# Row statistics of the second normalisation taken in the attention stage; the gelu output weighted by POOL and DVE, a tile each

## The reference

```
h = concatenate([tokens(x), text(x_txt)], axis=1)          # 64 x 228 x 192
h = h + attn(layernorm(h))
h = h + ffn(layernorm(h))

def ffn(x): return bitlinear(gelu(bitlinear(x, w1, g1)), w2, g2)
def bitlinear(x, w, g):
    xn = x * rsqrt(mean(x * x) + 1e-6) * g
    scale = 127 / max(max(|xn|), 1e-5)                    # one per row
    xq = clip(round(xn * scale), -128, 127) / scale
    return xq @ ternary(w)
```

## Time and profile before

| | |
|---|---|
| median of 3 runs | 1896.07 us |
| the profiled execution | 1889.4 us, of which the span from first to last instruction is 1887.7 us |
| busy, share of the span | PE 1579.8 us (84%), DVE 1364.8 (72%), ACT 1283.7 (68%), POOL 1089.7 (58%) |
| mean granted clock of TensorE | 0.880 of full speed (2.4 GHz) |

### The profile page before, as it was taken

One profiled execution on the slowest core, in us unless ns is written; L12 is line 12 of the kernel. 1 busy time (PEld: TensorE's weight loads), 2 busy tenths in 40 slices (PEclk: granted clock), 3 DMA queues, 4 the chain that ended last, 5 costly groups with the idle time before them and its releaser, 6 DMA issues.

```text
span 1887.7 us, 50796 instructions
## 1 busy us (share of the span) xinstructions
PE 1579.8 (84%) x16574; PEld 1297.6 (69%) x16574; DVE 1364.8 (72%) x3151; ACT 1283.7 (68%) x1958; POOL 1089.7 (58%) x1503
## 2 busy tenths in 40 slices
PE   0539999999999999999999999999466666666666
PEld 0427788888888888888888888887345555555555
DVE  3636676767767676767676767676389999999996
ACT  1226666766767676767676666665288888888887
POOL 5035555555555555555555555554177777777775
PEclk9869999999999999999999999999666666666665
DMA  8674666665657565756565666660000000000000
GB/s 102 141 127 59 95 87 96 86 99 83 103 79 104 83 99 83 99 88 94 89 94 91 91 93 88 94 87 25 17 16 21 21 21 22 22 22 22 22 22 26
DMA packets 159967, 132.96 MB, mean 70 GB/s; under 512 B 32558, under 2 KB 151040, under 8 KB 159808
## 3 DMA queue, kind: packets, MB, share of 16 engines
q1 hardware_dynamic: 159168, 131.00, 44.4%
q0 software_dynamic: 768, 1.57, 0.5%
HBM read 118.32 MB, written 11.91 MB: 69 GB/s over the span
## 4 chain that ended last, share of the span: by engine, by line
PE 66%; DVE 15%; issue 7%; SPq 3%; ACT 3%; DMA 3%; POOL 1%; DVEq 1%; ACTq 0%; POOLq 0%
PE ps L1092 20%; PE ps L1176 8%; PE ps L1259 7%; PE ps L1250 7%; PE ps L1206 4%; DVE ff_st L860 4%; PE ps L1238 3%; PE ps L1232 3%; PE ps L1211 3%; PE ps L1336 2%; PE ps L1355 2%; DVE xpix L841 2%; PE ps L1167 2%; DVE xpix L853 1%; PE ps L1157 1%
## 5 line engine op out<-in xcount | busy, mean ns | idle before, releaser
L1092 PE MATMUL ps<-w_eff,pix 118*112 118x193 f32 (+1 forms) x2048 | 408.4, 337 | 25.0 <-ACT pix L909 24.3
L927 ACT ACTIVATE probs<-ps,isw 116x688 f32<-116x688 f32 x384 | 299.2, 831 | 171.6 <-PE ps L1238 171.6
L527 POOL TENSOR_TENSOR xpix<-probs,g_b 112x192 f32<-112x192 f32 (+1 forms) x512 | 296.5, 609 | 109.1 <-ACT probs L1044 99.7
L741 DVE TENSOR_REDUCE nmax<-ps 116x12 bf16<-116x1344 f32 (+2 forms) x192 | 299.6, 1560 | 80.2 <-PE ps L1211 77.7
L452 POOL TENSOR_TENSOR xsq<-xsq 118x784 f32<-118x784 f32 (+2 forms) x192 | 221.8, 1155 | 218.5 <-ACT xsq L920 208.4
L1092 PEld LDWEIGHTS ps<-w_eff,pix 118*112 118x112 f32 (+1 forms) x2048 | 309.8, 167 | 52.4 <-issue 18.9
L472 POOL TENSOR_SCALAR_AFFINE_SELECT probs<-probs 116x464 f32<-116x464 f32 x384 | 268.2, 717 | 46.5 <-ACT probs L927 31.0
L909 ACT ACTIVATE pix<-xpix 118x896 f32<-118x896 f32 (+1 forms) x128 | 198.4, 1552 | 104.9 <-DMA xpix<-in_x 56.0
L457 POOL TENSOR_TENSOR front_st<-front_st,expo 128x2 f32<-128x2 f32 x64 | 45.0, 703 | 235.2 <-DVE front_st L693 221.2
L1336 PE MATMUL ps<-w1t,xpix 96*112 96x384 f16 (+1 forms) x512 | 160.7, 488 | 14.6 <-ACT xpix L1035 13.3
L685 DVE TENSOR_SCALAR front_st<-ps 112x1 f32<-112x1 f32 (+1 forms) x128 | 18.3, 151 | 213.8 <-PE ps L1157 202.4
(11 more groups left out here) (161 smaller groups left out, 3363.3 us busy)
## 6 DMA issues: line engine op xcount, KB each, us to landing
xpix<-in_x SPq DMA_DIRECT2D x192, 196.0 KB
xpix<-in_x SPq DMA_DIRECT2D x192, 195.1 KB
rden<-den_rows SPq DMA_DIRECT2D x256, 85.5 KB, 2.1
out<-xpix SPq DMA_DIRECT2D x64, 87.0 KB
out<-xpix SPq DMA_DIRECT2D x64, 84.0 KB
xpix<-in_x SPq DMA_DIRECT2D x128, 34.1 KB
xpix<-in_x SPq DMA_DIRECT2D x128, 34.0 KB
den<-o_sb SPq DMA_DIRECT2D x256, 2.7 KB
```

Source lines behind the costliest of these rows:

```text
L527: last = nc.gpsimd.tensor_tensor(v2[0:P, b, tile, cols], gel[0:P, b, tile, cols], g2_b[0:P, cols], ALU.mult)
L741: V.tensor_reduce(dst, src, AX_X, ALU.max, negate=True).then_inc(s_mx, 1)
L927: A(probs[0:TB, g, 2 * e:2 * e + 2, :], ps[0:TB, 4 + 2 * e:6 + 2 * e, 0:SK], ACT.Exp, scale=isw[0:TB, 7:8]).then_inc(s_p, 1)
L1092: last = MM(ps_tok[tile][0:P, :], src, w_eff[0:HI, o, :], start=(o == 0), stop=(o == OFFS - 1))
```

## The change

Four things:

1. The statistics of the second normalisation (mean, variance, peak) move from DVE's FFN step to DVE's attention step: a new function `measure(n - 1)` stands behind the third round of maxima. Mean, root and peak are kept for all images, two columns each. POOL takes the root in its own attention step (`row_roots`). Between the stages DVE makes `scale1` and `step1` of all images at once, in five instructions.
2. In the FFN stage DVE centres the rows again (`centre`) and quantises them with the kept scale.
3. The product of gelu and g2 of tile 0 goes from POOL to DVE (`weigh`); POOL keeps tile 1. The second quantisation of tile 1 goes from ACT to DVE (`quantise_second`); ACT keeps tile 0. POOL takes over the addition of epsilon to the mean squares (`gelu_roots`).
4. DVE's order in a step is now: centre i+1, final i-3, weigh i, peaks of i-1, quantise i+1, scales of i-1, quantise tile 1 of i-1.

Buffers move with it: `v1` uses the SBUF of `tok_t`, `bias_q` that of `aT`. The core of the diff:

```diff
+            def measure(n):
+                ...
+                dve.wait_ge(s_h2, n + 1)
+                apart(dve)
+                for tile, P in enumerate((TA, TB)):
+                    last = V.bn_stats(ln_st[0:P, 20 + 6 * tile:26 + 6 * tile], h_all[0:P, hcols(n, tile)])
+                chain(last, 1)
+                ...
+                after(dve, s_rms, n)
+                V.tensor_scalar(ln_st[:, 32:34], ln_st[:, 35:38:2], 1.0 + EPS_RMS,
+                                EPS_LN * EPS_RMS, ALU.mult, ALU.add).then_inc(s_var2, 1)
+                V.tensor_copy(mean2[:, bass.ds(n * 2, 2)], ln_st[:, 34:38:2])
+                for tile, P in enumerate((TA, TB)):
+                    last = V.scalar_tensor_tensor(v1[0:P, tile, :], h_all[0:P, hcols(n, tile)],
+                                                  ln_st[0:P, 34 + 2 * tile:35 + 2 * tile], g1_b[0:P, :],
+                                                  ALU.subtract, ALU.mult)
+                chain(last, 3)
+                for tile, P in enumerate((TA, TB)):
+                    last = V.tensor_reduce(peak[0:P, bass.ds(n * 2 + tile, 1)], v1[0:P, tile, :], AX_X, ALU.max,
+                                           apply_absolute_value=True)
+                last.then_inc(s_peak, 1)
...
+            link(V.tensor_tensor(peak[:, :], rms[:, :], peak[:, :], ALU.mult))
+            link(V.tensor_scalar(peak[:, :], peak[:, :], 1e-5, None, ALU.max))
+            link(V.reciprocal(inv_peak[:, :], peak[:, :]))
+            V.tensor_scalar(step1[:, :], peak[:, :], isw[:, 4:5], None, ALU.mult)
+            link(V.scalar_tensor_tensor(scale1[:, :], inv_peak[:, :], 127.0, rms[:, :], ALU.mult, ALU.mult))
...
+            def quantise_first(n):
+                dve.wait_ge(f_v1, n + 1)
+                after(dve, f_t1, n)
+                for tile, P in enumerate((TA, TB)):
+                    ins = V.tensor_scalar(q1[0:P, tile, :], v1[0:P, tile, :], scale1[0:P, bass.ds(n * 2 + tile, 1)],
+                                          MAGIC16, ALU.mult, ALU.add)
+                ins.then_inc(f_q1, 1)
...
+            def weigh(n, b):
+                for tile, P in ((0, TA),):
+                    after(dve, f_q2[tile], n - 1)
+                    dve.wait_ge(f_g, 2 * n + tile + 1)
+                    V.tensor_tensor(v2[0:P, b, tile, :], gel[0:P, b, tile, :], g2_b[0:P, :],
+                                    ALU.mult).then_inc(f_v2[tile], 1)
+
+            def peaks(n, b):
+                for tile, P in enumerate((TA, TB)):
+                    dve.wait_ge(f_v2[tile], n + 1)
+                    ins = V.tensor_reduce(ff_st[0:P, b, 26 + tile:27 + tile], v2[0:P, b, tile, :], AX_X, ALU.max,
+                                          apply_absolute_value=True)
...
+            def ffn_step(i, b, new=True, mid=True, last_=True, fresh=True):
+
+                if new:
+                    centre(i + 1)
+                if last_:
+                    final(i - 3, 1 - b)
+                if fresh:
+                    weigh(i, b)
                 if mid:
+                    peaks(i - 1, 1 - b)
+                if new:
+                    quantise_first(i + 1)
                 if mid:
+                    second_scales(i - 1, 1 - b)
+                    quantise_second(i - 1, 1 - b)
...
-                          scale=ff_st[0:P, b, 40 + tile:41 + tile]).then_inc(f_g, 1)
+                          scale=step1[0:P, bass.ds(m * 2 + tile, 1)]).then_inc(f_g, 1)
```

More of the change, by code:

```diff
@@ L240, in build @@
         f_sc = sem("quantiser_scales_ready")
[L241 to L242 removed]
+        f_v2 = [sem(f"gelu_weighted{i}") for i in range(2)]
+        f_q2 = [sem(f"second_quantised{i}") for i in range(2)]
         f_t2 = sem("second_transposed")
@@ L509, in _ @@
             step_images(IMAGES - 1, 0, None, newer=False, newest=False)
[L511 to L537, removed]
+            row_roots(IMAGES - 2)
+            row_roots(IMAGES - 1)
+            def weight(n, b):
+                after(pool, f_q2[1], n - 1)
+                pool.wait_ge(f_g, 2 * n + 2)
+                for lo in range(0, HIDDEN, HIDDEN // 4):
+                    cols = slice(lo, lo + HIDDEN // 4)
+                    last = nc.gpsimd.tensor_tensor(v2[0:TB, b, 1, cols], gel[0:TB, b, 1, cols],
+                                                   g2_b[0:TB, cols], ALU.mult)
+                last.then_inc(f_v2[1], 1)
@@ L569, in _ @@
             step(V.memset(nmax[:, :, :], 0.0))
+            for filled in (mean2, rms, peak):
+                step(V.memset(filled[:, :], 1.0))
             dve.wait_ge(s_const, 32)
@@ new lines, in final @@
+            def final(n, b):
+                dve.wait_ge(f_m2, n + 1)
+                after(dve, f_out, 32 * n)
+                for tile, P in enumerate((TA, TB)):
+                    end = V.scalar_tensor_tensor(y[0:P, tile, :], ps[0:P, 1, tile * 256:tile * 256 + DIM],
+                                                 ff_st[0:P, b, 42 + tile:43 + tile], h_all[0:P, hcols(n, tile)],
+                                                 ALU.mult, ALU.add)
+                end.then_inc(f_y, 1)
+            def weigh(n, b):
[4 more added lines that the diff above has]
+                                    ALU.mult).then_inc(f_v2[tile], 1)
@@ L1037, in ffn_step @@
                 if mid:
-                    quantise(i, b, 0)
-                    quantise(i, b, 1)
+                    quantise(j, 1 - b)
                 if new:
-                    after(act, f_v2, 2 * m - 2)
+                    for tile in range(2):
+                        after(act, f_v2[tile], m - 1)
                     for tile, P in enumerate((TA, TB)):
```

185 lines of the change are left out of this document (95 added, 90 removed).

## The result

The changed kernel takes 1919.65 us (median of 4 runs, 1912.34 to 1928.37), the kernel before 1897.02 on the same chip: ratio 1.0118, 95% interval 1.0066 to 1.0170. It is slower, as forecast (1924). The profiled execution is 1912.34 us, with a span of 1910.6 against 1887.7.

The account below looks back on a forecast made before the run. The prediction took PE to bound attention and DVE the FFN stage, where the change would close a chain of 8.4 us an image: + 26 us, + 2 for scales, giving 1917 profiled, 1924 median; own range 1905 to 1940, wider range 1882 to 1944.

Parts of the forecast that it names:

- What leaves DVE: FFN stage: second-normalisation statistics leave, a product and a quantisation come; DVE busy falls from 7.33 to 6.8 us an image.
- The closed chain: FFN stage: first quantisation, PE, gelu, weighing, peaks, next first quantisation form one loop; 8.4 us an image against 7.97.
- The correction to the mean clock: FFN chain: PE's parts taken at the stretch's mean times, lowering 8.60 us by 0.30 and 0.14 to 8.16.
- the 8.60 of the one image: FFN chain priced from one traced image, PE almost throughout at the lower clock: 4.75 + 0.98 + 0.95 + 1.92 us.
- The rival that the clock rises: FFN stage: PE at 2.4 GHz shortens the chain to 6.6 us, DVE's 7.2 bounds, 1850 us; chance 0.04.
- the rival above it: FFN stage: DVE stays the bound at 7.45 us an image, 1866 us; chance 0.18.
- The signs named beforehand: FFN profile: period 8.2 to 8.6 us, DVE about 80% busy waiting mainly on gelu, PE waiting for L883, longer ACT wait.
- No change: FFN stage: the chain comes out at the present period of 7.97 us, 1898 us; chance 0.08.
- DVE-bound: FFN stage: DVE's busy time and gaps still bound, so its lost work shows, 1866 us; chance 0.18.
- Contention: FFN stage: a 0.6 us POOL piece delays weighing or first quantisation, 1961 us; attention overrun alone 1936; chance 0.13.
- Attention hidden: Attention stage: DVE's added 2.8 us an image fits its 3.1 us idle time, 0.3 to spare; cost 0.
- The scales of all rows: End of the attention stage: five DVE instructions making scales for all images at once, not hidden, + 2 us.

Follow-up runs that it names:

- the order tests: The changed kernel with the first quantisation of image i+1 ahead of the weighing: 1824.85 us; with it between weighing and peaks: 1823.50 us.
- the doubled weighing: The changed kernel with DVE making the weighing product twice, first into memory nobody reads: 1989.42 us, ratio 1.0507.
- the doubled centring: The changed kernel with DVE centring image i+1 twice, first into memory nobody reads: 1926.63 us, ratio 1.0184.
- the first trace: Profile of the unaltered changed kernel in its first measurement of four runs; the profiled execution took 1912.34 us.
- the second trace of after: Profile of the unaltered changed kernel from its six later runs (median 1904.89 us); the traced run took 1926.25 us.
- one run of ten: Four first and six later runs of the unaltered changed kernel, 1855.47 to 1928.37 us; the one with clock 0.943 took 1855.5 us.
- TensorE kept busy: The changed kernel with eight idle matmuls at the end of every FFN step of TensorE: 1822.24 us, ratio 0.9630.
- the version with both tiles on POOL: The changed kernel with POOL weighing both gelu tiles and DVE none: 1888.49 us, ratio 0.9975.
- the statistics alone: The kernel before with the measuring piece and row root added in the attention stage, results unused: 1896.43 us, ratio 1.0024.

## Why the prediction was right, and where not

- **What leaves DVE.** Mostly right, and more left than I said: busy 279.70 / 46 = 6.1 us an image, not 6.8. The new pieces cost what was taken. What I missed is that DVE's time before held waiting for POOL: TENSOR_SCALARs of 128x2 and 128x4 took 415 and 484 ns (L831, L867), and one of 128x2 takes 169 (L916) now that POOL multiplies half as much.
- **The closed chain.** Right: the order tests, the doubled weighing against the doubled centring, and the waits show it. Its links: L883 to gelu 4.67 (4.75 forecast), gelu 1.00 (0.98), weighing 0.87 until the peaks start (0.95), peaks to the next L883 2.11 (1.92 + 0.13).
- **The correction to the mean clock.** This is the step that does not hold, though the number came out near. I took 0.44 us off the 8.60 of the one image, since the stretch had a mean clock of 0.65, and added 0.25 for two address computations: 8.4. No step has a mean length. One in which PE's part of the chain misses the higher level takes 8.53 us, one in which it has it 6.82, and the forecast of 8.4 lies between two lengths, at which nearly no step is. Without the correction the sum is 8.60 + 0.25 = 8.85, which is 0.3 too high for the long steps, mostly between L883 and gelu (4.62 on average over the long steps, not 4.75 + 0.13); the correction hid that. With long steps alone the stage grows by 0.56 x 61 = 34 us, and each short step takes 1.71 off. With the first trace's 11 short steps that makes + 15, with none + 34; measured, without the 2.2 us of the scales, the stage grew by 13.7 and by 31.3. My + 26 lies between, and that the median came near it is in part luck: it is the mixture of steps in those four runs.
- **The rival that the clock rises** was named at 4%, with the argument that a longer period makes PE idler. That argument failed: PE was busy for less (223.60 us against 255.50, and 232.40 in the second trace of after), and the clock was higher (0.76 and 0.70 against 0.65). It is the rival that I weighed most wrongly: it happened in 11 steps of after's first trace, by its mean clock (0.943) in much of the stage in one run of ten, and in every step with TensorE kept busy. Its time, 1850, was 28 us too high against the 1822 measured: I let DVE bound at 7.2 us an image (7.45 in the rival above it; the two do not agree), where DVE is busy for 321.86 / 55 = 5.9. The chain at the higher level, 6.6 in the forecast, measured 6.82.
- **The signs named beforehand.** DVE's largest wait is on gelu before L900, PE waits for L883 (151.4 us, 111.9 before), ACT waits longer for PE (67.6 us, 33.5 before): as said. DVE is busy for 75%, not 80. The period is 375 / 46 = 8.15 us in the stretch, a little under the 8.2 to 8.6 named. One sign of being wrong did appear, a clock well above 0.65; it means what the prediction said of it, that PE's part was overpriced, in the short steps, and the chain stands all the same.
- **No change, and DVE-bound:** neither came.
- **Contention** was small in after: L883's 386 ns against 311 is 0.15 us an image, some 9 us, in the place where I had taken none. As a mechanism it was right, and it is what spoils the version with both tiles on POOL.
- **Attention hidden:** DVE's wait before L702 fell from 168.1 to 20.3 us in 53 images, 0.38 each, as forecast (0.3). Still the statistics alone cost 1.5 to 7.4 us; where, stays open.
- **The scales of all rows:** from 1369.90 to 1372.12 in the trace, 2.2 us; forecast 2.
- **The range** of 1882 to 1944 holds nine of the ten runs.

## What to carry to other kernels

When work is moved to a faster or idler engine, follow one item around the loop and ask whether its result now comes back to the same engine's queue within a step: a closed chain costs its latency, however idle each engine is, and here the cure was the order of two pieces of work on one engine. Where TensorE's clock changes within a stretch, price a chain at each level and count steps, don't average. An engine that waits for another between two of its own pieces has room for a third one.

## What the hardware showed that I had not expected

- Adding 8 matmuls an image to TensorE (61.5 us of busy time in 375) made the kernel 83 to 97 us faster, by either median of after: the granted clock of the stretch went from 0.76 to 1.00. By the Trainium skill (TensorE: Matmul & The Clock Gate, Part 1) the throttle of the clock was seen at half and at full rate only in the three kernels looked at, never between; the twelve products of 2.13 and 1.15 us agree.
- The clock does not follow PE's busy time: 255.50 us busy at 0.65 in before, 223.60 at 0.76 in after, 277.72 at 0.75 with the quantisation moved ahead of the weighing, 237.72 at 1.00 with TensorE kept busy, all in the same 375 us.
- The same program ran in 1855 and in 1926 us on one chip, and the mean clock of the runs orders their times almost without exception.
- A product of 128x2 elements took 1440 ns on average beside POOL, and 151 in after.
